# Attention of all 32 half-heads from one list of steps: three two-bank score slots instead of a four-bank and a two-bank slot, and no loops

## The reference

```python
ct_q = x @ Wd_q_w + Wd_q_b
query = heads(ct_q @ Wu_q_w + Wu_q_b) + heads(_rope(ct_q @ Wq_r_w + Wq_r_b, cos, sin))
ct_kv = x @ Wd_kv_w + Wd_kv_b
key = heads(ct_kv @ Wu_k_w + Wu_k_b) + heads(_rope(x @ Wk_r_w + Wk_r_b, cos, sin))
value = heads(ct_kv @ Wu_v_w + Wu_v_b)
attn = softmax(einsum('bhqd,bhkd->bhqk', query, key) / scale)
out = einsum('bhqk,bhkd->bhqd', attn, value) @ Wo_w + Wo_b
x = layernorm(x + out)
x_int8 = clip(round(x / x_scale), -128, 127)      # x_scale from the largest |x|
x = layernorm(x + (x_int8 @ weight_int8.T) * x_scale * weight_scale.T + bias)
```

## Time and profile before

| what | us |
|---|---|
| median of three runs | 2140.95 (2139.43 to 2142.78) |
| profiled execution | 2142.55, its span 2140.7 |
| TensorE matmuls busy | 1881.4 (88%) |
| ScalarE busy | 1818.3 (85%) |
| VectorE busy | 1610.1 (75%) |
| GpSimd busy | 166.1 (8%) |
| first activation of the attention | at 158.6 |
| last activation of the attention ends | at 2055.9 |

### The profile page before, as it was taken

One profiled execution on the slowest core, in us unless ns is written; L12 is line 12 of the kernel. 1 busy time (PEld: TensorE's weight loads), 2 busy tenths in 40 slices (PEclk: granted clock), 3 DMA queues, 4 the chain that ended last, 5 costly groups with the idle time before them and its releaser, 6 DMA issues.

```text
span 2140.7 us, 35531 instructions
## 1 busy us (share of the span) xinstructions
PE 1881.4 (88%) x13009; PEld 429.9 (20%) x13009; DVE 1610.1 (75%) x1514; ACT 1818.3 (85%) x1418; POOL 166.1 (8%) x129
## 2 busy tenths in 40 slices
PE   8957999998998999899989899898989989898975
PEld 3331111111111111111111122111111111111134
DVE  3648877777777877787777766887897777777838
ACT  4445989899899989999999987899999999999955
POOL 5725200000000000000000000000030000000002
PEclk9987999999999999999999999999999999999997
DMA  5652111100011111111111001111100011111012
GB/s 187 204 186 85 23 23 22 22 19 16 13 18 22 22 22 22 22 22 22 22 26 54 16 11 23 23 24 23 21 16 15 18 20 22 22 22 23 8 33 79
DMA packets 165387, 80.10 MB, mean 37 GB/s; under 512 B 130204, under 2 KB 146716, under 8 KB 164856
## 3 DMA queue, kind: packets, MB, share of 16 engines
q1 hardware_dynamic: 164024, 78.11, 14.2%
q10 hardware_dynamic: 1312, 1.32, 0.2%
HBM read 48.83 MB, written 29.23 MB: 36 GB/s over the span
## 4 chain that ended last, share of the span: by engine, by line
PE 67%; ACT 15%; issue 7%; DVE 7%; DMA 1%; POOL 1%; SPq 1%; ACTq 0%; DVEq 0%; POOLq 0%
PE PS L539 39%; PE PS L502 24%; ACT arena L762 14%; PE PS L1017 2%; PE PS L604 1%; DVE arena L793 1%; DVE bn L692 1%; DMA Qst<-parts_or_sums 1%; DVE arena L816 1%; DVE parts_or_sums L772 1%; DVE parts_or_sums L777 1%; DVE parts_or_sums L770 0%; DVE arena L1621 0%; POOL arena L1340 0%; POOL arena L1339 0%
## 5 line engine op out<-in xcount | busy, mean ns | idle before, releaser
L762 ACT ACTIVATE arena<-PS 128x2048 f32<-128x2048 f32 (+1 forms) x1248 | 1712.0, 1443 | 197.1 <-PE PS L502 188.1
L539 PE MATMUL PS<-arena,Vh 128*32 128x512 f32 x8192 | 1106.7, 614 | 0.5 <-ACT arena L762 0.5
L502 PE MATMUL PS<-Qst,Kst 49*128 49x512 f16 x4096 | 716.4, 389 | 198.2 <-ACT arena L762 149.9
L816 DVE SCALAR_TENSOR_TENSOR arena<-arena 128x2048 f32<-128x2048 f32 x288 | 659.6, 2290 | 0.2
L793 DVE TENSOR_SCALAR arena<-PS 128x512 int32<-128x512 f32 x384 | 265.1, 690 | 395.2 <-PE PS L502 382.4
L502 PEld LDWEIGHTS PS<-Qst,Kst 49*128 49x128 f16 x4096 | 155.5, 94 | 1194.4 <-ACT arena L762 774.1
L539 PEld LDWEIGHTS PS<-arena,Vh 128*32 128x32 f32 x8192 | 163.7, 108 | 375.4 <-issue 373.6
L812 DVE SCALAR_TENSOR_TENSOR arena<-arena 128x2048 f32<-128x2048 f32 x96 | 220.4, 2296 | 0.0
L800 DVE TENSOR_SCALAR arena<-arena 128x2048 int32<-128x2048 int32 x96 | 118.7, 1237 | 9.5
L738 POOL TENSOR_TENSOR ctkv<-arena,rows 128x256 f32<-128x256 f32 x16 | 21.2, 1367 | 1334.1 <-DVE arena L719 1334.1
L802 DVE TENSOR_SCALAR arena<-arena 128x2048 int32<-128x2048 int32 x96 | 118.7, 1236 | 0.0
(11 more groups left out here) (104 smaller groups left out, 489.3 us busy)
## 6 DMA issues: line engine op xcount, KB each, us to landing
Kst<-k_halves SPq DMA_DIRECT2D x64, 128.0 KB
Qst<-q_halves SPq DMA_DIRECT2D x64, 128.0 KB
Vh<-head_values SPq DMA_DIRECT2D x30, 256.0 KB, 7.6
arena<-xT_dram SPq DMA_DIRECT2D x8, 512.0 KB, 5.4
k_halves<-parts_or_sums SPq DMA_DIRECT2D x16, 256.0 KB, 2.4
k_whole<-arena SPq DMA_DIRECT2D x8, 512.0 KB, 3.4
q_halves<-parts_or_sums SPq DMA_DIRECT2D x16, 256.0 KB, 3.4
q_whole<-arena SPq DMA_DIRECT2D x8, 512.0 KB, 4.4
```

Source lines behind the costliest of these rows:

```text
L502: return nc.tensor.matmul(out, Kst[par][low:low + HK + 1, at:at + 128], Qst[par][low:low + HK + 1, j * CH:(j + 1) * CH], start=True, stop= ...
L539: last = nc.tensor.matmul(PS[32 * j:32 * j + 32, OT * CH:(OT + 1) * CH], Vh[par][:, kt, :], moving, start=kt == first, stop=kt == last_kt)
L762: nc.scalar.activation(P[:, at * CH:(at + k) * CH], bank(SLOT_BANKS[g % 2][0], k), ACT.Exp, scale=EXP_SCALE).then_inc(a.exp, 1)
L816: last = nc.vector.scalar_tensor_tensor(out=t, in0=t, scalar=POLY[3 - j], in1=power if j == 3 else mantissa, op0=ALU.add, op1=ALU.mult)
```

## The change

One list of 1860 steps covers all 32 heads, and every engine's attention code is written out straight: no loop is left in it.

- A group is two blocks; there are three slots of two banks (banks 0 to 5), and TensorE writes the scores of group s+3 in step s. The ring stays at 24 blocks. ScalarE runs 62 + 31 x 58 = 1860 activations of 1024 columns.
- A step holds at most one value product. The value products of a head begin six steps after its first step (`HEAD_GAP = 6`), so steps 0 to 5 of every head hold none; then each goes into the first free step after its key tile is complete. The list that results for heads 1 to 30, in steps of the head: 6, 7, 8, 9, 11, 12, 13, 15, 16, 17, 19, 20, 23, 24, 27, 28, 31, 32, 33 or 34, 35, 36, 39, 40, 43, 44, 47, 48, 51, 52, 55, 56, 57.
- VectorE's blocks have steps of their own (one tile each 19.33 steps, blocks only in steps that are 1 modulo 3): 12 in a head, for example in its steps 1, 4, 10, 16, 19, 25, 28, 34, 40, 43, 49 and 55. Head 0 gives VectorE only key tile 15; there are 94 VectorE tiles instead of 96. The eight blocks ahead of the attention (`vector_begins`) are gone.
- The norm of a head is split: the copy of bank 7 comes behind the VectorE block in step 1 or 2 of the next head, the rest after the read of the next block.
- The first half's projection is one tile at a time, in 16 steps spread over some 300, four steps behind the fourth block of a VectorE tile; VectorE adds each between the two bit operations. Its statistics and normalisations are one operation behind a block each. The 16 inverse deviations are made by GpSimd with a power, so ScalarE's table is no longer changed within the attention. `check_range` and `ffn_weights` move to VectorE blocks 40 and 50.
- `bias_out` comes ahead of the first scores. SyncE's loads are the same in the same order, a head at a time.

```diff
-SLOT_BANKS = ((0, 4), (4, 2))
+FIRST_BY_VECTOR = (15,)
+SLOTS, SLOT = 3, 2
 D_BANK, OT = 6, 7
+RING = 24
+HEAD_BLOCKS = [head_blocks(t) for t in range(NT)]
+GROUPS = [(t, blocks[n:n + SLOT]) for t, blocks in enumerate(HEAD_BLOCKS) for n in range(0, len(blocks), SLOT)]
+PERIOD = (HEAD_STEP[2] - HEAD_STEP[1]) / len(BY_VECTOR)
+SPREAD, BLOCK_PHASE, VALUE_PHASE = 0.9, 1, 0
+HEAD_GAP = 6
+COPY_EARLY = 3
+def block_step(n):
+    c, j = divmod(n, QB)
+    s = START + int(c * PERIOD + j * PERIOD * SPREAD / QB)
+    while s % SLOTS != BLOCK_PHASE:
+        s += 1
+    return s
 def make_values():
+        ready = [(first + n // SLOT, kt) for n, (kt, j) in enumerate(HEAD_BLOCKS[t]) if j == QB - 1]
+        for kt in by_vector(t):
+            last = QB * TILES.index((t, kt)) + 2 * QB - 1
+            done = BLOCK_STEP[last] + 5 if last < len(BLOCK_STEP) else STEPS_ALL
+            ready.append((max(done, first + HEAD_GAP + 6), kt))
+        step = max(step, first + HEAD_GAP)
+        for g, kt in sorted(ready):
             step = max(step, g)
+            while step < STEPS_ALL and len(at[step]) == 1:
+                step += 1
+            at[min(step, STEPS_ALL)].append((t, kt))
+        step += 1
...
-            with nc.Fori(0, PROJECT_PAIR, engines=(pe.engine,), hint_back_edge=True) as i:
-                pair(i)
-            pair(PROJECT_PAIR, project=True)
-            with nc.Fori(PROJECT_PAIR + 1, PAIRS - 1, engines=(pe.engine,), hint_back_edge=True) as i:
-                pair(i)
-            pair(PAIRS - 1, more=False)
+            for g in range(SLOTS):
+                scores(g)
+            for s in range(STEPS_ALL + 1):
+                if s < STEPS_ALL:
+                    pe.wait_ge(a.exp, s + 1)
+                if s + SLOTS < STEPS_ALL:
+                    scores(s + SLOTS)
+                for n, at in enumerate(BLOCK_STEP):
+                    if at == s:
+                        block(n)
+                if s in PROJECT_STEP:
+                    project_first(PROJECT_STEP[s])
+                for t, kt in VALUES[s]:
+                    values(t, kt)
...
+        def attention_vector(dve, a, hooks):
+            copied = None
+            for c in range(CYCLES):
                 for j in range(QB):
+                    n = QB * c + j
+                    if j == 0 and c:
+                        dve.wait_ge(b_split, 2 * c)
+                    block_bits(dve, n, j)
+                    if copied is not None:
+                        norm_rest(dve, a, copied, copied // 2, copied % 2)
+                        copied = None
+                    if c:
+                        poly_step(dve, a, c - 1, j)
+                    if n in COPY_AFTER:
+                        copied = COPY_AFTER[n]
+                        norm_copy(dve, a, copied)
+                    if n in hooks:
+                        hooks[n]()
```

More of the change, by code:

```diff
@@ L53 @@
[L53 to L67, removed]
-def make_values():
[L72 to L81, removed]
+RING = 24
@@ new lines, in by_vector, with head_blocks @@
+def by_vector(t):
+    return BY_VECTOR if t else FIRST_BY_VECTOR
+def head_blocks(t):
+    low, high = ([kt for kt in half if kt not in by_vector(t)] for half in (range(UPPER), range(UPPER, KT)))
+    both = min(len(low), len(high))
+    blocks = [b for n in range(both) for j in range(QB) for b in ((low[n], j), (high[n], j))]
+    return blocks + [(kt, j) for kt in low[both:] + high[both:] for j in range(QB)]
+HEAD_BLOCKS = [head_blocks(t) for t in range(NT)]
+GROUPS = [(t, blocks[n:n + SLOT]) for t, blocks in enumerate(HEAD_BLOCKS) for n in range(0, len(blocks), SLOT)]
@@ L90, with ring_need @@
 VALUE_ORDER = [v for at in VALUES for v in at]
[L91 to L113, removed]
-HK = 3 * HD
-PROJECT_PAIR = 9
-STATS_PAIR = 10
-NORM_PAIR = 11
+assert [t for t, _ in VALUE_ORDER] == [t for t in range(NT) for _ in range(KT)]
+VALUE_COUNT = {v: n + 1 for n, v in enumerate(VALUE_ORDER)}
+VALUES_END = [max(s for s, at in enumerate(VALUES) if any(of == t for of, _ in at)) for t in range(NT)]
+def ring_need(g):
+    before = g - RING // SLOT
+    return max(VALUE_COUNT[GROUPS[before][0], kt] for kt, _ in GROUPS[before][1]) if before >= 0 else 0
+VALUES_FIRST = [min(s for s, at in enumerate(VALUES) if any(of == t for of, _ in at)) for t in range(NT)]
+COPY_AFTER = {max(n for n, s in enumerate(BLOCK_STEP) if s <= VALUES_FIRST[t + 1] - COPY_EARLY): t for t in range(NT - 1)}
+assert len(COPY_AFTER) == NT - 1
+HK = 3 * HD
+PROJECT_CYCLE = next(c for c in range(CYCLES) if BLOCK_STEP[QB * c + QB - 1] >= HEAD_STEP[TH + 1])
+PROJECT_STEP = {BLOCK_STEP[QB * (PROJECT_CYCLE + n) + QB - 1] + 4: n for n in range(TH)}
+STATS_BLOCK = QB * (PROJECT_CYCLE + TH)
+NORM_BLOCK = STATS_BLOCK + TH + 12
+assert len(PROJECT_STEP) == TH and NORM_BLOCK + TH + 8 < QB * CYCLES
 KR = 6 * HD
@@ L441, in build @@
         STACK_INC = 10 * 16
+        NOT_FIRST = [kt for kt in BY_VECTOR if kt not in FIRST_BY_VECTOR]
+        assert NOT_FIRST == list(range(KT - len(NOT_FIRST), KT))
+        ONES_ALL = 3 + len(by_vector(0)) + len(by_vector(1)) + 1
         def load_values(sp, s, t, par):
@@ L469, in attention_sync @@
         def attention_sync(sp, a, first, end):
[L470 to L477, removed]
+            for t in range(first, end):
+                par = t % 2
+                sp.wait_ge(a.qk, QK0 + HEAD_STEP[t + 1])
+                load_stack(sp, a.stack[par], t + 2, par)
+                load_shift(sp, a.stack[par], t + 2, par)
+                store_head(sp, a, t, t, par)
+                load_values(sp, a.vh[par], t + 2, par)
         def load_heads(sp, a, half, parts):
@@ L516, in cycle_block, with block @@
[L516 to L530, removed]
-                vector = kt in BY_VECTOR
+            def block(n):
+                c, j = divmod(n, QB)
+                t, kt = TILES[c]
+                if j == 0 and kt == by_vector(t)[0]:
+                    pe.wait_ge(a.stack[t % 2], STACK_INC * (t // 2 + 1))
+                if j == 0 and PROJECT_CYCLE < c <= PROJECT_CYCLE + TH:
+                    pe.wait_ge(p_added, c - PROJECT_CYCLE)
+                if n:
+                    pe.wait_ge(b_bits, n)
+                score_block(bank(D_BANK), t % 2, kt, j).then_inc(b_qk, 1)
```

287 lines of the change are left out of this document (122 added, 165 removed).

## The result

| what | before | after |
|---|---|---|
| median, us | 2140.19 (2139.43 to 2142.78) | 2104.32 (2102.67 to 2106.47) |
| profiled execution, its span | 2142.55, 2140.7 | 2106.47, 2104.6 |
| last exponential of the attention ends | 2055.8 | 2019.7 |

The ratio is 0.9831, interval 0.9814 to 0.9848. The forecast was 2088: the direction and the mechanism held, and 16 us of the expected 53 did not come.

What follows compares the result with a forecast made beforehand. TensorE and ScalarE, each nearly full, wait for one another through two slots. Head 0's end at 220 + 31 x 57.0, + 12.5 + 4 - 1, + 84.8 tail gives span 2087.3; forecast 2088 us, range 2025 to 2140.

Steps and rivals of the forecast that it cites:

- ScalarE's step: ScalarE's 1024-column activations start 0.90 us apart, so a head of 58 steps needs 52.2 us.
- Rivals 2 and 3: ScalarE's step is longer: 0.95 us, total 2128 (chance 0.08); or 1.04, no overlap, total 2212 (chance 0.04).
- The lead of three slots: Score slots: a turn takes 1.6 us, three slots give 2.70; TensorE may be 1.1 late before ScalarE stands still.
- The list of steps: TensorE's lateness counted step by step against ScalarE's pace: overrun 3.3 us, a head 55.5 at full clock.
- The clock in the gap: TensorE's clock falls in the 4.6 us without value products, nine heads of ten: 1.45 us a head, bounds 0 and 3.2.
- VectorE's copy: Copy of bank 7 near step 6: 0 to 0.3 us of wait, hidden behind the gap; upper bound 2.3 a head.
- Rival 4: Low clock over steps 6 to 12 plus VectorE's order: 60.2 us a head, total 2188, slower; chance 0.07.
- rival 5: TensorE and ScalarE overlap better than listed: 53 us a head, no clock cost, total 1964; chance 0.04.
- Side work: Projection 12.5 us, range check and weights 4, within the attention: 16.5 together.
- Rival 6: Side work swallows the gain, costing 55 us beyond the 16.5; chance 0.03.
- Start and tail: ScalarE starts at about 158.1, head 0 is over at 220, the tail stays 84.8 us.
- the first: The clock does not fall in the new gap: 45 us less, total 2043; chance 0.16.

Runs made afterwards that it cites:

- e2: The changed kernel with two slots of two banks instead of three: 2341.18 us, ratio 1.0929 to the kernel before.
- e5: The changed kernel with VectorE's value products moved: tile 15 to step 8, tiles 30 and 31 to steps 21 and 37: 2102.88 us.
- e4: The changed kernel with a four-step gap, COPY_EARLY 2, and the copy of bank 7 ahead of the polynomial step: 2033.72 us.
- e6: The changed kernel with a four-step gap, the copy ahead of the polynomial step, and VectorE's tiles' products moved: 2033.90 us.
- e8: The changed kernel with a three-step gap, COPY_EARLY 1, early copy, moved products, and a bias wait before head 0's first value product: 2035.36 us.
- e3: The changed kernel with a four-step gap and COPY_EARLY 2, the copy still behind the polynomial step: 2127.64 us.
- e1: The changed kernel with score pairs computed twice in steps 0 to 5 of heads 1 to 31: 2087.68 us.
- e10: The changed kernel with a four-step gap, early copy, and score pairs of steps 0 to 3 of each head computed twice: 2041.71 us.

## Why the prediction was right, and where it missed

**ScalarE's step.** Put at 0.90; the median distance of the 1860 starts is 0.904. Rivals 2 and 3 (0.95, 1.04) are out. The fixed time of an activation and the overlap of neighbours that the Trainium skill gives ("ScalarE: Activation LUTs", "What ACT_TABLE_LOAD costs") are there in kind, but the estimate of 0.946 made from them is too long for this case: the overlap here is 0.13, not 0.09.

**The lead of three slots.** Put at 1.1 us of lateness. e2 takes the slot away: 64.7 a head and more, falls included, instead of 55.85 to 56.69 at full clock.

**The list of steps.** This was the part most worth testing. In heads 5, 11 and 14, adding up what each start-to-start distance exceeds 0.904 by:

| TensorE's steps | forecast | measured |
|---|---|---|
| 6 to 20 | 2.6 | 2.4 |
| 31 to 40 | 0.4 | 0.5 |
| 55 to 57 | 0.3 | 0.4 |
| a head | 55.5 | 55.85 |

58 x 0.904 + 3.4 = 55.85. The forecast counted four VectorE blocks in steps 6 to 20; there are three, and with three the same sum gives the measured 2.4. But it took one head for all. The list has three kinds, and every third head is 0.8 longer (56.69), since two of VectorE's products fall into steps 14 and 37 there. The average at full clock is 56.2, and that is the term of the sum that was most off.

How far the list can be trusted shows when other orders are walked with the same numbers: 0.42 up for a product, 0.68 down without one, 0.22 up for a block, never below zero, and all above 1.1 is overrun. The measured overrun is a head at full clock less 58 x 0.904. The three values are the three kinds of heads in turn:

| order | walked | measured |
|---|---|---|
| changed kernel | 3.5, 3.5, 4.0 | 3.5, 3.4, 4.3 |
| e5, products moved | 3.5, 3.5, 4.0 | 3.5, 3.4, 4.1 |
| e4, four steps | 2.6, 2.6, 2.6 | 2.0, 2.2, 4.1 |
| e6, four steps, moved | 2.7, 2.7, 2.9 | 2.5, 2.6, 3.1 |
| e8, three steps, moved | 2.0, 2.0, 2.2 | 2.6, 2.4, 2.6 |

So the list already says that e5 gains nothing, and that a head still takes 54.4 to 55.3 with three or four steps. It is up to 0.6 off either way, too long for e4 and too short for e8. The one large miss, e4's third head, holds the wait of 1.2 for tile 30, which is not in the list. Only the sentence that without the gap TensorE's 51.0 would fit under 52.2 was wrong: it compared totals, where the lead of 1.1 is all that carries a run of products over to the empty steps behind it.

**The clock in the gap.** The place, the length of the gap (4.6) and the mechanism were right. Forecast: 28 falls at 1.6, together 45 us. Measured: heads 1 to 31 take 2019.7 - 218.8 = 1800.9; less their lengths at full clock (11 x 55.95 + 10 x 55.85 + 10 x 56.69 = 1740.9) and 17.5 of side work, some 42 are left for 23 falls, 1.8 each (head 26's wait of 2.3 for the copy is still among them). In plain heads a fall costs 1.3 to 1.8 where it is short, as forecast from pair 14, and 2.5 to 3.1 where it lasts twice as long (heads 10, 15, 24, 27). That the sum came out so near is in part luck: there were fewer falls than expected, and a third of them were longer.

**VectorE's copy.** "It hides behind the gap; without the gap it would show whole": with six steps TensorE waits for it 4.0 us in all, with four 52.2 (e3). It shows with four steps only because the copy stands behind the polynomial step: with the copy ahead (e4) no head waits over 0.3 us for it. The upper bound of one polynomial step a head was the right size. Rival 4 needed this wait in every head and is out; so is rival 5, as no head takes under 55.8.

**Side work.** Put at 16.5. It can be read at full clock in e4, whose plain heads repeat 54.47, 54.67 and 56.58: heads 17 to 22 exceed their pattern by 2.7, 2.4, 3.1, 2.7, 2.4 and 0.9, head 4, with the weights, by 1.0, and head 26, with one of the two searches for the largest value, by 2.3; the range check in head 3 costs nothing that shows. Sum 17.5. So the range check and the weights took 1 of the 4 us put down for them, and the first half's work 16.5 instead of 12.5. Rival 6 is out.

**Start and tail.** The first activation came at 158.00 (forecast 158.1), head 0 was over at 218.8 (220), the tail took 84.9 (84.8). The straight code brought 103 instruction packets instead of 31, and no stall of it is to be seen.

```profile
158.00 4.69 ACT L747 ACTIVATE arena<-PS 128x1024 f32<-128x1024 f32 x5 [10.37 <-PE PS L513]
...
2011.04 8.65 ACT L747 ACTIVATE arena<-PS 128x1024 f32<-128x1024 f32 x9
2019.70 1.28 ACT L1239 ACT_TABLE_LOAD   x1
```

**The account.** Forecast span 2087.3, measured 2104.6, difference 17. Heads at full clock: 1740.9 - 31 x 55.5 = 20 too long. Of these 7 are ScalarE's step (0.904, not 0.90), 8 the third kind of head, and 5 the rest of the overrun. Falls: 42 - 45 = -3. Side work 1; the 1 us put down as saved in the last head, 1; start -1, tail 0; the rest is rounding. So the step that failed in size is the 55.5 for a head at full clock, not the clock. No mechanism of the sum was missing, but one sum hid another: at full clock a head went from about 57.15, which is (115.9 - 1.6) / 2, to 56.2, and 23 falls instead of 15, some of them longer, gave most of that back.

Of the rivals, the first (no fall, 2043) was the one to act on. With six steps of gap and no fall this kernel would take an estimated 2104 - 42 = 2062; e4, which also shortens the heads, takes 2034.

## What to carry to other kernels

Where TensorE has a short stretch of light work in every round, look at the granted clock behind it, and try the length of that stretch as a parameter: here 8, 6, 5 and 4 steps gave 2165, 2096, 2063 and 2034 us. A gap can hide a second wait; here it had to be shortened together with what it hid (e3 against e4), or the test would have misled. Counting each engine's gain and loss against the slower one's pace, step by step, gave the length of a head to about 1% in the average of its three kinds. It is worth walking a new order through the same count, for every kind of head, before building it: that would have said beforehand that e5 gains nothing.

## What the runs showed of the hardware that I had not expected

- The clock can fall although TensorE is not idle: in the gap it is at work in every step, with waits of 0.3 to 0.5 us between. The same gap is followed by a fall in some heads and not in others.
- More matmuls made a kernel faster: e1 does six steps of scores twice and is 17 us quicker, with 9 falls instead of 23. Where there was no fall to save (e10), the same trick cost 8 to 9 us.
- With four steps no head fell under the given list of products (e4), but four did under e5's list (e6), and five with three steps (e8). The gap's length alone does not settle it.
